# Transposes of a feed-forward tile in two blocks of eight instead of four blocks of four

## The reference

```python
x = x + 0.5 * ffn(layernorm(x))
x = x + mixer(layernorm(x))
x = x + 0.5 * ffn(layernorm(x))

def ffn(x):                                # itself normalises and adds a residual
    h = (x - mean) * rsqrt(var + EPS) * gamma + beta
    y = silu(h @ dequant(q1, s1) + b1)     # 256 -> 1024, scales for each 128 rows of q1
    return x + 0.5 * (y @ dequant(q2, s2) + b2)   # 1024 -> 256, scales for each 128 rows of q2
```

## Time and profile before

| | us |
|---|---|
| median of 3 runs (689.08 to 690.64) | 690.57 |
| the profiled execution | 690.4 |
| its span in the profile | 687.6 |
| outside the span | 2.8 |
| PE busy | 668.0 (97% of the span) |
| ACT busy | 653.4 (95%) |
| DVE busy | 634.8 (92%) |
| POOL busy | 604.8 (88%) |

### The profile page before, as it was taken

One profiled execution on the slowest core, in us unless ns is written; L12 is line 12 of the kernel. 1 busy time (PEld: TensorE's weight loads), 2 busy tenths in 40 slices (PEclk: granted clock), 3 DMA queues, 4 the chain that ended last, 5 costly groups with the idle time before them and its releaser, 6 DMA issues.

```text
span 687.6 us, 13669 instructions
## 1 busy us (share of the span) xinstructions
PE 668.0 (97%) x3224; PEld 539.2 (78%) x3224; DVE 634.8 (92%) x1329; ACT 653.4 (95%) x1095; POOL 604.8 (88%) x673
## 2 busy tenths in 40 slices
PE   3999999999999999999999999999999999999997
PEld 3678888888888878778877887788888888888885
DVE  5789999999999999889999998899999999999987
ACT  4899999999999999889999999999999999999994
POOL 4899999999999999857766789999999999999973
PEclk9999999999999999999999999999999999999999
DMA  8670000000000000000000000000000000000001
GB/s 254 172 236 4 1 0 0 0 0 0 0 0 0 1 0 2 1 1 1 0 0 0 0 1 1 30 33 32 31 31 31 31 31 31 31 31 32 32 32 63
DMA packets 19962, 20.22 MB, mean 29 GB/s; under 512 B 1564, under 2 KB 19666, under 8 KB 19922
## 3 DMA queue, kind: packets, MB, share of 16 engines
q1 hardware_dynamic: 19824, 19.74, 9.3%
q10 hardware_dynamic: 98, 0.02, 0.0%
HBM read 11.37 MB, written 8.39 MB: 29 GB/s over the span
## 4 chain that ended last, share of the span: by engine, by line
PE 90%; ACT 3%; DVE 3%; issue 2%; DMA 1%; ACTq 0%; POOL 0%; DVEq 0%; POOLq 0%
PE ps_z L1009 38%; PE ps_fc L1009 33%; PE ps_fc L1142 8%; PE ps_tr L1002 5%; PE ps_tr L1070 4%; PE ps_fc L1150 2%; PE ps_z L1002 1%; DMA rows<-in_L_attn_bc 1%; DVE z_acc L762 1%; ACT ps_fc L576 1%; ACT g_hi L593 1%; DVE stats L699 1%; ACT g_full L591 0%; DVE resid L887 0%; ACTq L530 0%
## 5 line engine op out<-in xcount | busy, mean ns | idle before, releaser
L410 POOL TENSOR_TENSOR g_lo<-g_full,g_hi 128x512 fp32r<-128x512 f32 x256 | 332.9, 1300 | 24.7 <-ACT g_hi L593 21.8
L762 DVE SCALAR_TENSOR_TENSOR z_acc<-ps_z,cols,z_acc 128x512 f32<-128x512 f32 (+1 forms) x449 | 322.2, 742 | 24.2 <-PE ps_z L1009 16.4
L1009 PE MATMUL ps_fc<-h_hi,q_sb 128*128 128x512 f32 x512 | 213.4, 417 | 1.4 <-ACT ps_fc L576 1.4
L1009 PE MATMUL ps_z<-g_hi,q_sb 128*128 128x512 f32 x512 | 202.4, 395 | 0.1
L1009 PE MATMUL ps_fc<-h_lo,q_sb 128*128 128x512 f32 x512 | 202.3, 395 | 0.0
L1009 PE MATMUL ps_z<-g_lo,q_sb 128*128 128x512 f32 x512 | 200.6, 392 | 0.0
L591 ACT ACTIVATE g_full<-ps_fc,safe_scale 128x512 f32<-128x512 f32 x256 | 194.8, 761 | 3.9 <-PE ps_fc L1009 2.2
L593 ACT ACTIVATE g_hi<-ps_fc,safe_scale 128x512 fp32r<-128x512 f32 x256 | 196.2, 766 | 0.0
L576 ACT ACTIVATE ps_fc<-ps_fc,bias,ratio 128x512 f32<-128x512 f32 x193 | 157.9, 819 | 1.8 <-DVE bias L873 1.8
L1009 PEld LDWEIGHTS ps_z<-g_hi,q_sb 128*128 128x128 f32 x512 | 96.1, 188 | 25.0 <-DVE z_acc L762 2.7
L1009 PEld LDWEIGHTS ps_fc<-h_hi,q_sb 128*128 128x128 f32 x512 | 97.3, 190 | 21.0 <-ACT ps_fc L576 2.1
(11 more groups left out here) (110 smaller groups left out, 820.4 us busy)
## 6 DMA issues: line engine op xcount, KB each, us to landing
resid<-in_L_attn_x SPq DMA_DIRECT2D x15, 512.0 KB, 4.6
out_x<-resid SPq DMA_DIRECT2D x15, 512.0 KB, 2.9
q_int<-in_L_ffn_fc_q SPq DMA_DIRECT2D x4, 512.0 KB, 7.3
resid<-in_L_attn_x SPq DMA_DIRECT2D x2, 256.0 KB, 3.0
out_x<-resid SPq DMA_DIRECT2D x2, 256.0 KB, 2.7
wd_sb<-in_L_attn_Wd SPq DMA_DIRECT2D x1, 256.0 KB
wy_raw<-in_L_attn_Wy SPq DMA_DIRECT2D x2, 64.0 KB
bias_rows<-in_L_attn_by SPq DMA_DIRECT2D x1, 128.0 KB
```

What stands on the lines that cost most here:

```text
L410: nc.gpsimd.tensor_tensor(g_lo[:, g % 4, :], g_full[:, g % 4, :], g_hi[:, g % 4, :].bitcast(F32), ALU.subtract).then_inc(g_ready, 1)
L762: nc.vector.scalar_tensor_tensor(out=z, in0=bank_of(g, n, par)[:, tokens], scalar=col(R_S2 + KC * g + n), in1=z, op0=ALU.mult, op1=ALU.add ...
L1009: last = nc.tensor.matmul(out, w, v, start=start and i == 0, stop=stop and i == len(pairs) - 1, skip_group_check=not start)
```

## The change

Behind slot 1, PE turns both halves of the next tile at once (eight transposes): c = 0 into bank 3 of `ps_fc1`, which is lent, and c = 1 into `ps_tr`. Behind slot 5 it turns both halves of z back at once: half 0 into bank 0 of `ps_fc1`, half 1 into `ps_tr`. The slots use the banks of `ps_fc1` in a new order (`GROUP_BANK`), and PE's waits for `silu` follow it (`SILUS_BEFORE`). ACT rounds c = 0 in slot 1 behind `silu(0)` and c = 1 in slot 2 ahead of `silu(1)`. DVE lowers c = 0 in slot 2 ahead of `add_group(6)`, and c = 1 in slot 3 ahead of `add_group(7)`; its `add_ffn` move to slots 6 and 7. POOL does the third quarter of `xhat` ahead of `g_low(6)` in slot 7 (`early`). The first tile of a layer keeps its four blocks, and the last tile of the second feed-forward layer its two of `turn_back`. The statistics, `BANKS` and the order of the matmuls are as before.

```diff
-    TURN_AT = ((3, 5), (2, 6), (2, 6))
-    TURN_OUT_AT = ((3, 5), (2, 6), (2, 6))
-    H_LOWER_AT = ((4, 6), (3, 7), (3, 7))
-    XN_LOWER_AT = (3, 7)
-    TURN_BACK_AT = ((), (4, 5), (4, 5))
-    ADD_AT = ((), (5, 6), (5, 6))
+    GROUP_BANK = (0, 1, 2, 0, 3, 1, 2, 3)
+    SILUS_BEFORE = (-4, -2, -1, 1, 0, 2, 3, 5)
+    FIRST_TURN_AT, FIRST_LOWER_AT = (3, 5), (4, 6)
+    TURN_AT, LOWER_AT = 1, (2, 3)
+    XN_LOWER_AT = (3, 4)
+    TURN_BACK_AT = 5
+    ADD_AT = (6, 7)
+    LAST_TURN_BACK_AT, LAST_ADD_AT = (4, 5), (5, 6)
...
-        back_banks = (ps_tr[:, :], ps_fc1[:, 0, :])
+        turn_banks = (ps_fc1[:, 3, :], ps_tr[:, :])
+        back_banks = (ps_fc1[:, 0, :], ps_tr[:, :])
...
+                        early = before and f == FC - 1 and (behind >= 2 or ff0 == 0)
+                        if early:
+                            normalise(ln + 2, t + 2 if behind >= 2 else 1 - behind, par, normalise_at[f], True)
                         if f >= 1:
                             g_low(ff, f - 1, par)
...
                         if f in on_act(ff):
                             scale_half(ff, f)
+                        if before and f == TURN_AT + 1:
+                            take_turned(t, ff, ln, par, behind, 1)
...
                             silu(ff, f - 1, par)
...
+                        if before and f == TURN_AT:
+                            take_turned(t, ff, ln, par, behind, 0)
...
+                        if before and behind and f == LOWER_AT[1]:
+                            lower_h(ln + 1, ff + 1, 1 - par, 1, turn_banks[1])
                         if f in on_dve(ff):
                             scale_half(ff, f)
+                        if before and behind and f == LOWER_AT[0]:
+                            lower_h(ln + 1, ff + 1, 1 - par, 0, turn_banks[0])
                         here = f >= LAG
                         if before or here:
                             add_group(ff if here else ff - 1, (f - LAG) % FC, par if here else 1 - par)
...
-                wait(pe, g_hi_ready, FC * ff + (f - 3))
+                wait(pe, g_hi_ready, FC * ff + SILUS_BEFORE[f])
...
+                        if before and turns and f == LAG:
+                            pe.wait_ge(turned_out, 2 * ln + 3)
                         half_products(ff, ln, f, par)
...
+                        if before and turns and f == TURN_AT:
+                            if before == 2:
+                                pe.wait_ge(ffn_added, 2 * ff - 2)
+                            pe.wait_ge(g_hi_ready, FC * ff)
+                            for c in range(KC):
+                                turn(ln + 1, 1 - par, c, turn_banks[c], 2, share(ln + 1, ff0))
...
+                        elif before and turns and f == TURN_BACK_AT:
+                            pe.wait_ge(g_hi_ready, FC * ff + LAG)
+                            pe.wait_ge(turned_out, 2 * ln + 4)
+                            for half in range(2):
+                                turn_back(ff - 1, 1 - par, half, back_banks[half])
```

More of the change, by code:

```diff
@@ L489, in tile @@
                                 rsqrt(ln + 2, par, twice, share(ln + 1, ff0))
-                            if f in normalise_at:
+                            if f in normalise_at and not early:
                                 normalise(ln + 2, t2, par, normalise_at[f], f == FC - 1)
@@ L611, in feed_forward, with take_turned @@
             def feed_forward(ff0, ln0):
+                def take_turned(t, ff, ln, par, behind, c):
+                    if behind:
+                        round_h(ln + 1, ff + 1, 1 - par, c, turn_banks[c])
+                    elif ff0 == 0:
+                        turn_out(0, 0, c, bank=turn_banks[c])
                 def tile(t, par, before, behind):
@@ L624, in tile @@
                             silu(ff - 1, FC - 1, 1 - par)
[L625 to L630, removed]
+                        if before and f == TURN_AT:
+                            take_turned(t, ff, ln, par, behind, 0)
+                        if not before and f in FIRST_TURN_AT:
+                            round_h(ln + 1, ff + 1, 1 - par, FIRST_TURN_AT.index(f))
                         if f == LAG:
@@ L778, in tile @@
                     for f in range(FC):
-                        if f in ADD_AT[before]:
-                            add_ffn(ff - 1, t - 1, ADD_AT[before].index(f))
+                        last = ff0 and not behind
+                        add_at = LAST_ADD_AT if last else ADD_AT
+                        if before and f in add_at:
+                            half = add_at.index(f)
+                            add_ffn(ff - 1, t - 1, half, ps_tr[:, :] if last else back_banks[half])
+                        if before and behind and f == LOWER_AT[1]:
+                            lower_h(ln + 1, ff + 1, 1 - par, 1, turn_banks[1])
                         if f in on_dve(ff):
                             scale_half(ff, f)
+                        if before and behind and f == LOWER_AT[0]:
+                            lower_h(ln + 1, ff + 1, 1 - par, 0, turn_banks[0])
                         here = f >= LAG
@@ L787, in tile @@
                             add_group(ff if here else ff - 1, (f - LAG) % FC, par if here else 1 - par)
-                        if behind and f in H_LOWER_AT[before]:
-                            lower_h(ln + 1, ff + 1, 1 - par, H_LOWER_AT[before].index(f))
+                        if not before and f in FIRST_LOWER_AT:
+                            lower_h(ln + 1, ff + 1, 1 - par, FIRST_LOWER_AT.index(f))
                         if ff0 and not before and f == 0:
@@ L1076, in tile @@
                     ff, ln = t + ff0, t + ln0
+                    turns = behind or ff0 == 0
                     for f in range(FC):
+                        if before == 2 and f == 0:
+                            pe.wait_ge(ffn_added, 2 * ff - 3)
+                        if before and turns and f == LAG:
+                            pe.wait_ge(turned_out, 2 * ln + 3)
                         half_products(ff, ln, f, par)
```

41 lines of the change are left out of this document (18 added, 23 removed).

## The result

The kernel after the change takes 714.64 us (median of 4 runs, 714.43 to 715.23), the kernel before 690.11 (4 runs, 689.08 to 690.64). The ratio is 1.0358, with a 95% interval of 1.0343 to 1.0374: slower by 24.5 us. The forecast was 713.5, in a range of 699 to 722.

What follows compares the result with a forecast made beforehand. PE bound the kernel, with ACT, POOL and DVE close behind. Steady tiles +21.6, tile 14 of the last layer +0.6, tile 15 +1, tiles 1 gaining 0.1: +23.1 on 690.4, so 713.5 us, range 699 to 722.

Steps and rivals of the forecast that it cites:

- all four links: Steady tiles, from silu(5): round_h at 7.05, lower_h at 7.89, group 7's first addition at 11.17, PE's bank at 11.96 us.
- rival 1: Steady tiles: DVE's own work, not ACT, sets lower_h; +9.3 us, about 700 us; chance 0.12.
- rival 3: Steady tiles: group 7's additions don't reach PE's path; gain of 0.06 in 29 tiles, 688.7 us; chance 0.10.
- The tiles: Steady tiles of both layers: even ones 17.71 us (+1.30), odd ones 16.80 (+0.39), 21.6 us over 13 even and 12 odd.
- PE's own gain: Each tile on PE: two blocks of eight transposes make it 16.35 us, a gain of 0.06, bounds 0 and 0.10.
- The price of a block of eight: Eight transposes on PE: 0.88 us, read from the mixer, against 0.91 for two blocks of four.
- the weight load saved at the block's end: Behind PE's transpose blocks: joining blocks saves part of the weight load, given as the source of the 0.06 us.
- Edits costed at nothing: Lent bank 3, scale_half(4), turn-back, third quarter of xhat, g_low(6), DMA and stores: each put down at no cost.
- The wait of the lent bank for silu(7): PE's block behind slot 1: silu(7) at about X + 5.4, needed at X + 5.73; any loss comes off fc2's wait.
- Rival 2: Odd tiles: PE stalls again at scale_half(4), longer in even ones; about 25 x 0.4, 723.5 us; chance 0.10.
- The tiles 1 gain 0.1: Tile 1 of the first layer and of the second feed-forward layer: together a gain of 0.1 us.
- Tile 15 of the first layer: The first layer's last tile: four copies on ACT in place of two roundings, +1 us, bounds 0 and 2.

Runs made afterwards that it cites:

- e3: The kernel after, with one more ACT instruction (an activation of 128x256 into an unread buffer) in slot 7: 728.1 us, ratio 1.0561 to the kernel before.
- e1: The kernel after, with the second pair of statistics moved to slot 4, behind the additions of group 7: 704.57 us, ratio 1.0221 to the kernel before.
- e2: The kernel after, with the break in the round of three banks moved to group 2 of even tiles: 703.28 us, ratio 1.0195 to the kernel before.
- e15: e12 with the turn-back's half in ps_tr first, silu(3) awaited only ahead of the other half: 690.28 us, ratio 1.0009 to the kernel before.
- e4: The kernel after, with the third quarter of xhat on POOL back behind g_low(6): 715.09 us, ratio 1.0373 to the kernel before.
- e14: e12 with PE's waits for silu first again, as in the kernel after: 697.97 us, ratio 1.0124 to the kernel before.
- e11: e9 with XN_LOWER_AT back at slots 3 and 7, as before the change: 706.73 us, ratio 1.0247 to the kernel before.
- e12: e11 with the statistics in slots 0 and 1 and lower_h ahead of its slot's additions: 692.78 us, ratio 1.0046 to the kernel before.
- e9: The kernel after, with group 6 ahead of lower_h, second lower_h and two statistics in slot 4, PE's silu wait last: 707.83 us, ratio 1.0258.

## Why the prediction was right

**The bound and the mechanism.** ACT's backlog, then two `lower_h` and the statistics ahead of group 7 on DVE, then the broken bank round: all four links were met within 0.04 us. e3 shows the first (ACT longer, both tiles longer), e1 the second, e2 the third. e3 also rules out rival 1, as does DVE's idle 0.53 us ahead of `lower_h` (the sum of that rival is 9.5 and not 9.3, which changes nothing); rival 3, the one on the other side, fell with the stall itself.

**The tiles.** 17.71 and 16.80 were forecast, 17.74 and 16.82 measured; the steady tiles of both layers cost 21.05 us where 21.6 were put down.

**PE's own gain.** The price of a block of eight, 0.88, was right, and e15 shows 0.06 us a tile. But that this is the weight load saved at the block's end isn't borne out. On average over tiles 2 to 11, a block of four with the matmul ahead and two behind spans 0.902 us before, not 0.91, and a block of eight 1.338 in e15. As 56 other steps between matmuls become 60, joining saves 4 x 0.902 - 2 x 1.338 - 4 x 0.2285 = 0.02 us a tile. The other 0.04 comes from those steps, which take 0.2281 us in e15 and 0.2289 before; no run shows why. So the size of this term was met by luck. The Trainium skill (TensorE: Matmul & The Clock Gate, Part 2: What happens when you issue a matmul) says that PE pulls a weight load ahead of matmuls in flight; by that the gain would be nothing if the load at a block's end were wholly hidden. The blocks' own 0.02 is near to that, though the matmul behind a block still stands 0.31 ahead of the next (151.34 - 151.03) where others have 0.228.

**Edits costed at nothing.** The third quarter of `xhat` is shown to be worth nothing (e4). The wait of the lent bank for silu(7) was covered; in e3, with ACT later, it appears (7.1 us in 19 waits of PE) and takes its time from the stall behind it, as the forecast said. What wasn't foreseen is the price of the waits themselves: some 0.17 us a block (0.12 ahead of it, the rest between its halves), hidden under the stall in the kernel after, 5.2 us in all where the stall is gone (e14). That it didn't show is luck: in the odd tiles of e1, whose stall is gone, it does.

**Rival 2** came in on a small scale: the cover of 0.1 us that was worked out for `scale_half(4)` was a little too short, and the weight load behind it stood idle for some 0.17 us in 12 tiles, not 0.4 in 25.

**The terms that were mis-sized.** "The tiles 1 gain 0.1" is wrong: they cost 0.84 and 0.93. The step left out was to ask of tile 1 what was asked of the steady tiles, when the last quarter of `xhat` is there for a block that goes one slot forward. The rows had it, 1.01 us of slack against 1.83. "Tile 15 of the first layer ... +1, bounds 0 and 2" was 2.37: the four copies were seen, but `XN_LOWER_AT`, which moves POOL's lowering ahead of `rstd`, was not followed along POOL's queue; e11 shows that it is worth 0.55 us in the trace (1.1 in the medians). Even without it tile 15 costs 1.65 more than before (e15), above the 1 put down, and no run shows why. These terms are 0.90 + 0.99 + 1.37 = 3.3 us too low and the steady tiles 0.5 too high, which makes the 25.8 us of span against 23.1. The profiled execution took 715.23 us, so 1.8 lie outside the span in place of 2.8, and that gives 1.0 back. That the forecast of 713.5 came within 1.2 us of 714.64 owes something to errors that offset each other: 3.3 too low in the edges, 0.5 and 1.0 too high elsewhere, and a median 0.6 below the profiled execution.

## What to carry to other kernels

Here, merging small blocks saved 0.06 us a tile on the engine that is full, some 0.02 of it at the blocks themselves, and it asks another queue to deliver earlier: before it is done, follow each producer from a fixed point of the loop, with every instruction queued ahead of it, to the buffer that the full engine needs next. Here 21.9 of the 24.5 us lost came back by moving work that nobody waits for (the statistics) into the time in which DVE was idle anyway (its additions' waits for PE fall from 26.5 us in the kernel after to 7.0 in e12), putting the second `lower_h` behind the additions, setting the wait that ends last behind all others, and (1.1 of it) taking a lowering back out of POOL's way. Do the same reckoning for the first and the last tile, whose queues hold other work than the steady ones.

## What the runs showed that was not expected

- **The order of waits on one engine costs time.** Ahead of a block PE's list holds several waits; when the first of them is the late one, the fulfilled ones behind it still take 0.12 to 0.14 us of PE's time ahead of each block (0.35 and 0.37 us between starts in place of 0.23), and the second half's some 0.05 inside it. With the late one last they lie beside PE's running matmuls: 697.97 against 692.78 us.
- **A tiny DVE operation can last as long as a large POOL one.** DVE's `tensor_scalar` on four columns took 1.11 us beside `g_lo` of POOL in e9 and 0.50 in the same tile of e12, where it stands elsewhere among POOL's instructions. Both times its end fell 0.02 us behind that of POOL's `g_lo`.
- **A wait that is removed is often another's cover.** e4 added 3.9 us of waits without adding time, and e9 took issue waits away without winning any. Of the sums by wait only the one that ends last in a tile tells what an edit is worth.
